# Causal attention: on SyncE's queue, the writes of the pair five ahead ahead of the skewed reads of the pair four ahead

## The reference

```python
q, k, v = heads(layernorm(x) @ Wq.T + bq), heads(ctx @ Wk.T + bk), heads(ctx @ Wv.T + bv)
QEr  = einsum('bhsd,ld->bhsl', q, Er)        # 512 x 512 for each head
Srel = skew(QEr)                             # row s is shifted left by 511 - s
attn = (q @ k.T + Srel) / 4
attn = softmax(where(causal, attn, -inf))
x    = x + attn @ v
```

## Time and profile before

| | us |
|---|---|
| median of 3 runs | 1245.04 (1243.53 to 1252.52) |
| profiled execution | 1249.81 |
| its span, first to last instruction | 1248.0 |
| causal attention's first and last soft work | 70.56 to 386.43 |
| mean granted TensorE clock, share of full | 0.917 |

### The profile page before, as it was taken

How to read it: one execution, slowest core, us unless ns; L and a number is a source line. 1 busy time by engine, 2 the same in 40 slices (tenths; PEclk the granted TensorE clock), 3 DMA queues, 4 the chain that set the end, 5 groups by cost and what they waited for, 6 DMA issues and landing times. The chain is left out here.

```text
span 1248.0 us, 22010 instructions
## 1 busy us (share of the span) xinstructions
PE 1090.8 (87%) x6978; PEld 676.4 (54%) x6979; DVE 661.8 (53%) x1993; ACT 637.4 (51%) x1275; POOL 199.1 (16%) x466
## 2 busy tenths in 40 slices
PE   7999989999998869899999995447999999997487
PEld 5556555555554549799999894212333333334344
DVE  4427776666766661121111110866766666684697
ACT  2456666667652323223332221425777777763687
POOL 0000000000000012133222220002222322240232
PEclk9958899999889889899999998668999999998699
DMA  5088888888785843677666662454111111110001
GB/s 177 15 279 259 273 258 255 266 264 277 259 263 185 319 161 118 229 226 233 221 223 230 212 209 75 155 198 123 45 49 46 45 49 45 45 32 9 0 29 40
DMA packets 75342, 199.55 MB, mean 160 GB/s; under 512 B 7880, under 2 KB 40904, under 8 KB 69256
## 3 DMA queue, kind: packets, MB, share of 16 engines
q1 hardware_dynamic: 71528, 188.45, 46.8%
q0 software_dynamic: 3744, 10.23, 2.2%
HBM read 134.82 MB, written 63.83 MB: 159 GB/s over the span
## 5 line engine op out<-in xcount | busy, mean ns | idle before, releaser
L784 DVE CUSTOM_DVE_ANT_0 unused<-mpsS,mask_bias 128x512 bf16<-128x512 f32 x256 | 172.0, 691 | 82.8 <-PE mpsS L717 82.4
L1526 ACT ACTIVATE hT<-ph,w 128x128 f32<-128x128 f32 x312 | 89.0, 368 | 207.1 <-PE ph L1500 179.9
L811 ACT ACTIVATE mPT<-mpsB 128x512 f32<-128x512 f32 x256 | 152.6, 597 | 80.9 <-PE mpsB L724 74.8
L1500 PE MATMUL ph<-xT,w 128*128 128x128 f32 x1248 | 152.2, 282 | 6.7 <-DMA w<-in_w1p 6.4
L1500 PEld LDWEIGHTS ph<-xT,w 128*128 128x128 f32 x1248 | 147.6, 198 | 9.7 <-issue 9.6
L1545 DVE TENSOR_TENSOR xn<-py,b 128x256 f32<-128x256 f32 x39 | 16.6, 425 | 246.3 <-PE py L1510 246.3
L1510 PE MATMUL py<-w,hT 128*128 x624 | 141.2, 379 | 0.7 <-DVE xn L1545 0.7
L659 ACT ACTIVATE scores<-scores,nm 128x512 f32<-128x512 f32 (+3 forms) x256 | 125.6, 557 | 12.5 <-DVE nm L624 12.5
L1510 PEld LDWEIGHTS py<-w,hT 128*128 128x128 f32 x624 | 115.6, 190 | 15.2 <-issue 1.1
L611 DVE CUSTOM_DVE_ANT_0 scores<-psS,bias 128x512 f32<-128x512 f32 (+3 forms) x176 | 79.1, 488 | 80.7 <-PE psS L552 56.2
L717 PE MATMUL mpsS<-mqk 96*128 96x512 bf16 x256 | 100.5, 394 | 19.8 <-DMA mqk<-packed 16.6
(11 more groups left out here) (267 smaller groups left out, 1662.1 us busy)
## 6 DMA issues: line engine op xcount, KB each, us to landing
w<-in_w1p SPq DMA_DIRECT2D x39, 1028.0 KB, 5.6
rel<-stage SPq DMA_DIRECT2D x44, 640.0 KB, 8.4
bias<-rel SPq DMA_DIRECT2D x44, 640.0 KB, 5.4
x<-rel SPq DMA_DIRECT2D x20, 640.0 KB, 4.8
mqk<-packed SPq DMA_DIRECT2D x64, 192.0 KB
w<-in_w2p SPq DMA_DIRECT2D x8, 1024.0 KB, 12.9
rel<-x SPq DMA_DIRECT2D x10, 640.0 KB, 7.9
rel<-mask_bias SPq DMA_DIRECT2D x10, 640.0 KB, 9.0
```

What stands on the lines that cost most here:

```text
L784: nc.vector.tensor_tensor_reduce(out=unused[:, i, :], in0=psS[i % 2][:, :], in1=mask_bias[:, i, :], scale=1.0, scalar=-3.0e38, op0=ALU.add ...
L811: nc.scalar.activation(PT[r][:, j, :], psB[j % 2][:, :], ACT.Exp, scale=1.0 / 4).then_inc(s_exp, 1)
L1500: mm = nc.tensor.matmul(ph[half][:, q * P:(q + 1) * P], w1[i][:, dk * F + f * P:dk * F + (f + 1) * P], xT[i][:, dk, :], start=(dk == 0), s ...
L1526: g = nc.scalar.activation(hT[i][:, f, :], ph[half][:, q * P:(q + 1) * P], ACT.Gelu, bias=w1[i][:, DK * F + f:DK * F + f + 1])
```

## The change

In each step SyncE's loop calls `write` for the pair five ahead before it calls `read` for the pair four ahead. All waits, counts, tensors and DMAs stay as they are, and so does the code of every other engine. In the first step (n = -5) there is only a write, from n = -4 to 26 there are both, and in the last three (n = 27 to 29) there is a read at 27 alone.

```diff
                     for n in range(-REL, NP - SOFT):
+                        if (p := pair_at(n, REL)) is not None:
+                            write(p)
                         if (p := pair_at(n, READ)) is not None:
                             read(p)
-                        if (p := pair_at(n, REL)) is not None:
-                            write(p)
                     for m in range(NBH - ROUND, NBH):
                         sp.wait_ge(s_wr[m % ROUND], 16 * (m // ROUND + 1))
```

## The result

The changed kernel runs in 1204.15 us (median of 4, 1203.68 to 1207.36) against 1246.73 of the kernel before (median of 4, 1243.53 to 1252.52): ratio 0.966, 95% interval 0.962 to 0.970, 42.6 us less. It lies in the range on record (1200 to 1234) and 7 us under the forecast. The profiled execution took 1203.75 us, its span is 1202.0, against 1248.0 before.

A forecast was written before the change was run, and what follows sets the result against it. SyncE's queue was taken to stand behind its own DMAs, each next write behind a read awaiting a landing. Stalls 35, less 5 left, plus clock 7, less start 3, give 34 us: from 1245.0 to 1211, range 1200 to 1234.

The forecast's parts named there:

- What is removed: SyncE's wait of each write for the previous write's landing; 35.0 us of VectorE bias waits gained over 28 steps.
- Stalls that stay: VectorE's waits for late biases left in the 28 steps: 5 us, with bounds of 0 and 15.
- L: Time from ScalarE's last evacuation of the next pair to the landing of head 1's read: 10 to 10.5 us.
- the need: How long after the next pair's last evacuation VectorE needs head 1's bias: 10.3 to 11.5 us.
- The clock: TensorE's granted clock, 0.93 in the 28 steps, partly recovers without stalls: 7 us gained, half of 13.4.
- rival (a): Clock stays full and no stalls are left in the stage: up to 45 us gained, 1200 us; chance 0.10.
- 13.4 us: Time in the 28 steps above 8.2 us each after stalls are taken off, put down to the clock; return open.
- The start: First read goes about 2 us later, behind the write of pair 1: 3 us lost, bounds 0 and 4.
- The end: Last read has no write ahead of it and the weights' loads wait as before: no change.
- (b): Half the gain: DMA engines (floor 8.1 us a step) or TensorE take over as the bound, 1229 us; chance 0.18.
- (c): Slower: reads, now last of four transfers, land later than VectorE takes them, 1271 us; chance 0.09.
- (d): The change does nothing: writes are issued no sooner, or another wait takes up the 35 us, 1245 us; chance 0.06.

The follow-up runs named there:

- e2: Changed kernel with the old read-before-write order from step n = 11 on, the new order before it: 1226.30 us.
- e5: Changed kernel with the writes issued from ScalarE's queue and only the reads left on SyncE's: 1203.01 us, ratio 0.965 to the kernel before.
- e7: Changed kernel in which each read also waits until the next pair's two writes, issued just ahead of it, have landed: 1255.55 us.
- e6: Changed kernel with four useless VectorE copies of 128x512 ahead of head 1's first soft tile from pair 16 on, no DMA changed: 1244.79 us.
- e0: The changed kernel run again unaltered, with a second trace: 1204.82 us, ratio 0.966 to the kernel before.
- e1: Changed kernel with only the very first read (pair 0) put ahead of the write of pair 1: 1201.57 us, ratio 0.963 to the kernel before.
- e4: Changed kernel with each stage written a second time to a scratch nobody reads, six transfers a pair instead of four: 1264.51 us.
- e3: Changed kernel with the reads one pair later, three ahead instead of four (READ 3): 1455.18 us.

## Why the prediction was right, and where its sizes were off

**What is removed.** Right. The wait for landings left the loop that carries the steps, and VectorE's 35.0 us of DMA waits went to nothing between T(3) and T(31). e2 puts it in the steady steps, e5 shows that another way of freeing the write does it as well, and in e7, where fresh landings are waited for again, the gain is gone, though the writes stand ahead of the reads in the text.

**Stalls that stay: 5 us forecast, 0 measured.** "Just in time" was right in kind. The landing L of head 1's read behind E was taken as 10 to 10.5 us, from the writes' median as the last of four in a row. In the trace after it is 8.5 to 10.6 us over the pairs 3 to 30, median 9.5, and the need, put at 10.3 to 11.5, is 10.7 us or more. The least room was 0.4 us (pair 20). So the stalls were avoided by little: with L half a microsecond longer some would have been there.

**The clock: 7 us forecast, 14.1 measured.** This is the step that was mis-sized. 278.0 - 228.9 = 49.1 us, 35.0 of them stalls; the rest, 14.1, is what the half clock had cost, and all of it came back (0.93 to 1.00). The trace before bears this out step by step. Of its 28 steps 18 had the full clock throughout; with their DMA waits taken off, they last what the same steps last after the change, to 0.2 us each. All the rest lies in the ten steps whose clock was 0.68 to 0.95. One of each kind, T(10) to T(11) and T(20) to T(21):

```profile
168.34:178.40 10.06, 9.30 (x82) 5.26 (x81) 6.66 (x20) 6.08 (x12) 0.00 (x0) 1.00 0.86 269
268.21:280.50 12.29, 10.79 (x82) 5.97 (x81) 6.60 (x21) 6.39 (x15) 0.00 (x0) 0.86 0.80 257
```

With head 1's waits for the bias taken off (1.79 and 2.74 us) they last 8.27 and 9.55 us; both last 8.39 after the change.

I gave rival (a), which is what happened (full clock, no stalls, 1200), a chance of 0.10, because one stretch with a stall of 1.94 us kept its full clock. That reading asked too little of the row: it shows that a stall need not be followed by a drop, not that drops come without stalls. e6 makes them out of stalls alone, e2 has them only in its stalled half. A given stall still does not tell: thirteen steps of the kernel before with 0.8 to 2.3 us of DMA wait kept the full clock. The Trainium skill, TensorE: Matmul & The Clock Gate, section "HAM oscillation — how this bites in real kernels", says that waits which idle TensorE bring the throttle back. By it all 13.4 us would have come back, and the sum would have been 1204 to 1205; the trace after agrees (1.00).

**The start: 3 us forecast.** Head 1 of pair 0 began at 74.95 instead of 72.00, as forecast to a tenth (about 75). How much of these 2.95 us is left at T(3) differs from trace to trace of the same code: 1.15 us in the first, where the clock between 96 and 104 us was 0.96, and 2.96 in e0, where it was 0.61. e1, which takes the cost away, gains 3.2 in the median. So 3 was a fair size.

**The end: nothing forecast,** 1.95 us lost after T(31) in the first trace. In e0 the same code took 868.2 us from there to the end, 0.3 more than before: the 1.95 are the spread of executions, not the change.

**The rivals.** (a) is what happened. (b) falls by e4 and by the steps themselves: TensorE's busy row of 259 us was not solid work, since the same 2130 matmuls are busy 222.8 us at full clock without stalls. Its L of 13 us was put without a working from the floor of 8.1. (c) names a real edge, and it is not far: one pair later costs 251 us (e3), 80 more than the expected 171, with a clock of 0.71. (d) fell with the first row after.

The sum as it came out: 35.0 + 14.1 - 1.15 - 1.95 = 46.0 us between the two spans and 42.6 between the medians, against 34 forecast. The time, 1204.15, lies at the lower edge of the forecast's own 1204 to 1222: the mechanism was right, and that both open terms, stalls left and clock, came out at their favourable end was not foreseen.

## What to carry to other kernels

In an in-order queue that stores and then reloads the same data, look for a load that waits on a landing while an independent store stands behind it: the period of the loop is then landing plus issue, even where the engines could go faster. Put the store that is ready ahead, with a step between each store and its load, or give the two their own queues, and check in the trace by how much each load still beats its user. When stalls go from a stage bound by TensorE, count the clock that comes back with them.

## What the runs showed of the hardware

- SyncE's issue of a read took 0.32 us in the kernel before (319 ns median) and 0.85 us right behind two fresh writes in the changed kernel (854 ns median, 2.6 us at most). In e7, where those writes have landed first, it is 0.32 us again (320 ns median): the same instruction holds the queue longer when the writes just ahead of it are still going.
- Writes and skewed reads of 640 KB with 5120-byte rows moved at 382 GB/s over 282 us (e4), with the DMA engines at 0.97; 422 in the best 2 us before.
- A busy share of the DMA engines of 0.82 left room for 20% more bytes in the same time (264 to 316 GB/s) at 0.87.
- TensorE's granted clock fell in some of the steps with stalls of about 2 us: 0.96 in e2's second half, 0.90 in e6 from T(16) on. Without such stalls it stayed at 1.00 over all 28 steps in two traces of the changed kernel; in e5 it fell once, in the last two steps.
